# Attention loop of a block chain on one core: score matmuls ahead of the maximum ring, whole value sums, the shift in four tiles

## The chip, the core and the metric

The kernel runs on one core of a Trainium2 chip. TensorE (PE in the profile, PEld for its weight loads) multiplies, VectorE (DVE) reduces and normalises, ScalarE (ACT) applies exponentials and moves tiles out of PSUM, GpSimd (POOL) and SyncE (SP) do the rest. The metric is the time of one execution on the device in microseconds; lower is better. The median of three runs of the kernel before is 976.74 us (974.82 to 978.44).

## The reference

Eight residual blocks in a row work on x of 2 x 1024 tokens by 128 channels, in float32. The change touches only the softmax attention with rotary positions, 16 heads of 8 channels:

```
x_norm = layer_norm(x, g1, beta1)
q = (x_norm @ Wq + bq).reshape(B, S, H, hd).transpose(0, 2, 1, 3)
k = (x_norm @ Wk + bk).reshape(B, S, H, hd).transpose(0, 2, 1, 3)
v = (x_norm @ Wv + bv).reshape(B, S, H, hd).transpose(0, 2, 1, 3)
q = apply_rope(q); k = apply_rope(k)
q = q * (1.0 / jnp.sqrt(jnp.float32(hd)))
scores = jnp.einsum('bhqd,bhkd->bhqk', q, k)
attn = jax.nn.softmax(scores, axis=-1)
out = jnp.einsum('bhqk,bhkd->bhqd', attn, v)
...
x = x + attn_out
```

The other blocks (linear attention, two channel mixes, a top-2 and two top-1 expert layers, a linear memory) are the same in both kernels.

## The kernel before: how the attention loop is laid out

The class is SoftmaxAttention. Its work is cut into 16 **halves** (HALVES): one batch, one group of 4 heads (HG) and 512 queries each. A half runs through 8 **waves** (kt, 0 to 7), one for each tile of 128 keys. A wave k has these parts:

- **Scores.** Four matmuls (score, L1674), one for each head j = 0 to 3, of 32 rows of the array (rows 32j to 32j+31) and 512 columns in f16. Score tiles go round three PSUM banks (SCORE_BANKS, banks 4 to 6). score_bank makes PE wait on prob_in until ScalarE has read the tile three places earlier in the stream of tiles. stream_tiles numbers them: s0, s1, s2, s3 of each wave, and the shift tiles between.
- **Exponentials.** ScalarE turns each score tile into probabilities (L1871), in order, and raises prob_in after each. Before a wave's first one it waits on wave_in until the buffer of three waves earlier (PROBS) has been summed.
- **Value sum.** wave (L1705) multiplies the probabilities of wave k - 2 (BEHIND) with the values, in float32, into bank 7: four heads side by side in column groups of 32. Before, it is done in two parts of 256 columns, one after scores 0 and 1, the other after scores 2 and 3; for kt = 0 it is one piece of 512.
- **The maximum ring.** For the softmax each query's maximum over the keys is found in advance, one half ahead. ring_fill (L1614) computes the scores of 128 queries against 1024 keys of one head by two matmuls of 512 columns into one of two slots (banks 0 and 1, or 2 and 3); VectorE reduces a slot (L1634) and raises ring_out. An item may be filled only when VectorE has read the item two places earlier. A half has 16 items, in the order of fills(), and the loop fills two a wave, AHEAD = 4 items in front. Items of kind "o" transpose finished outputs (L1640), two tiles each, and are read by a reciprocal and a multiplication; there are four of them.
- **The shift.** shift subtracts the maxima from the queries: in a score bank one f16 copy of 512 columns (L1684) and four float32 matmuls of 128 columns (L1686, two passes each). ScalarE moves the result to qT2 (L1858). Before, that is done once a half, after wave kt = 6 (SHIFT_AT).
- **The sum's move.** After wave kt = 1 ScalarE copies the last half's sum out of bank 7 (move_sum, L1853); the first value sum of a half waits for it.

PE runs its instructions in the order that loop_tensor writes out. In it a wave is: ring item, s0, s1, first part of the sum, ring item, s2, s3, second part of the sum. keep_busy issues dummy matmuls (L287) whose results nobody reads. Ahead of the loop PE fills 2 ring items, then eight times one dummy, eight small transposes (turn_split, L1723) and 2 ring items. In the last half the transposes and projections of batch 0 and the late outputs of batch 1 are put between the waves.

## Time and profile before

| what | value |
|---|---|
| median of 3 runs | 976.74 us (974.82 to 978.44) |
| the profiled execution | 985.43 us, of which 983.5 us are its span |
| attention loop, from the first exponential to the last | 377.2 to 708.7 us of the span |
| TensorE busy | 861.3 us (88%) |
| VectorE busy | 665.9 us (68%) |
| ScalarE busy | 558.2 us (57%) |

In the profile a start is in us from the span's start, and a row of the timeline has its start, the time that it covers, engine, line, operation, output and input, shapes and the count of merged instructions; what stands in brackets is the engine's idle time ahead of it and who ended that. A matmul in float32 has two rows, one for each pass. Matmuls in different row groups of 32 can run side by side, so that durations overlap: what counts is the distance between starts.

### The profile page before, as it was taken

The page shows a single profiled execution, that of the slowest core. Times are in us where ns is not written, and L with a number is a line of the kernel's source. Part 1 is how long each engine was busy: PE and PEld are TensorE (multiplying, and loading weights), DVE is VectorE, ACT ScalarE, POOL GpSimd, SP SyncE. Part 2 cuts the span into 40 slices and gives each one's busy share as a digit, 9 for nine tenths or more (in the row PEclk, how much of TensorE's full clock was granted, in tenths as well). Part 3 has the DMA queues.
Part 4 walks back from the last instruction along what each step waited for, and adds up shares of the span by engine and source line. Part 5 has one row for each costly group of instructions (what it writes and reads, how often), then busy time and mean ns, then how long its engine had stood idle before and what let it go on. Part 6 is the DMA issues. An engine that isn't in the chain of part 4 may idle for free.

```text
span 983.5 us, 17217 instructions
## 1 busy us (share of the span) xinstructions
PE 861.3 (88%) x6571; PEld 536.4 (55%) x6571; DVE 665.9 (68%) x1248; ACT 558.2 (57%) x1188; POOL 198.1 (20%) x177
## 2 busy tenths in 40 slices
PE   4889935899988689999999999999996899895894
PEld 2579733599855443333333333333465599594694
DVE  5845882366487988999999888896335354566362
ACT  2442532165534836999989877889754055324152
POOL 2000047255400040000000000000030645104385
PEclk9999957999999968999999999999998799995798
DMA  5740001411120000000000000000060121100434
GB/s 118 201 129 1 2 19 51 123 37 34 42 80 1 1 1 1 2 1 2 1 1 2 2 2 1 1 2 1 2 172 2 61 69 37 43 2 25 125 34 70
DMA packets 54643, 36.86 MB, mean 37 GB/s; under 512 B 9138, under 2 KB 50162, under 8 KB 54546
## 3 DMA queue, kind: packets, MB, share of 16 engines
q1 hardware_dynamic: 47218, 25.98, 9.5%
q0 software_dynamic: 7344, 9.77, 4.3%
q8 instruction: 53, 0.87, 0.4%
q14 instruction: 28, 0.23, 0.1%
HBM read 22.31 MB, written 14.48 MB: 37 GB/s over the span
## 4 chain that ended last, share of the span: by engine, by line
PE 46%; DVE 20%; issue 19%; POOL 8%; DMA 3%; ACT 3%; SPq 1%; POOLq 0%; DVEq 0%; ACTq 0%
PE psum L1705 10%; DVE arena L1634 10%; PE psum L1614 8%; POOL results L1158 5%; PE psum L287 4%; PE psum L1674 3%; POOL results L1169 2%; PE psum L1251 2%; PE psum L402 2%; PE psum L380 2%; POOL slots L1147 2%; PE psum L1686 2%; PE psum L1766 1%; PE psum L1754 1%; PE psum L440 1%
## 5 line engine op out<-in xcount | busy, mean ns | idle before, releaser
L1634 DVE TENSOR_REDUCE arena<-psum 128x1 f32<-128x1024 f32 x256 | 296.8, 1219 | 33.9 <-PE psum L1614 30.8
L1871 ACT ACTIVATE arena<-psum 128x512 f32<-128x512 f32 x512 | 273.0, 599 | 32.9 <-PE psum L1674 24.5
L1294 ACT ACTIVATE arena<-psum,arena 128x128 f32<-128x128 f32 x340 | 96.9, 368 | 123.3 <-PE psum L1261 66.1
L1614 PE MATMUL psum<-arena 32*128 32x512 f16 x512 | 152.5, 388 | 8.3 <-ACT arena L1986 4.5
L1705 PE MATMUL psum<-arena 128*32 128x256 f32 (+1 forms) x1920 | 159.4, 405 | 0.2 <-ACT expert_w L1853 0.2
L1674 PE MATMUL psum<-arena 32*128 32x512 f16 x512 | 150.0, 385 | 0.5 <-ACT arena L1871 0.5
L287 PE MATMUL psum<-la_wqkv,ident 128*128 128x384 f32 x308 | 117.3, 532 | 7.2 <-issue 6.5
L1147 POOL DMA_INDIRECT slots<-xn,arena x64 | 66.3, 1036 | 196.1 <-DVE arena L1371 177.5
L1251 PE MATMUL psum<-arena 128*128 128x128 f32 x680 | 96.2, 286 | 1.4 <-DVE arena L1452 1.3
L287 PEld LDWEIGHTS psum<-la_wqkv,ident 128*128 128x128 f32 x308 | 60.9, 206 | 58.5 <-issue 25.6
L1261 PE MATMUL psum<-arena 128*128 128x128 f32 x680 | 90.4, 276 | 1.0 <-issue 0.7
L1251 PEld LDWEIGHTS psum<-arena 128*128 128x128 f32 x680 | 85.5, 197 | 4.7 <-DVE arena L1452 3.3
L1442 DVE COPY arena<-expert_w 128x1028 f32 x85 | 60.8, 715 | 35.9 <-issue 34.9
L1261 PEld LDWEIGHTS psum<-arena 128*128 128x128 f32 x680 | 83.4, 193 | 1.6 <-issue 1.1
L1614 PEld LDWEIGHTS psum<-arena 32*128 32x128 f16 x512 | 28.4, 93 | 101.8 <-DVE arena L1634 71.3
L1158 POOL DMA_INDIRECT results<-arena x62 | 61.6, 994 | 80.4 <-DVE arena L1457 78.6
L2158 POOL TENSOR_TENSOR x<-x,xn 128x1024 f32<-128x1024 f32 x2 | 4.7, 2358 | 362.6 <-DVE arena L2133 362.6
L1705 PEld LDWEIGHTS psum<-arena 128*32 128x32 f32 x1920 | 38.2, 108 | 71.5 <-issue 62.1
L1674 PEld LDWEIGHTS psum<-arena 32*128 32x128 f16 x512 | 42.3, 91 | 44.9 <-ACT arena L1871 32.3
L1457 DVE TENSOR_SCALAR arena<-psum,arena 128x128 f32<-128x128 f32 x85 | 29.8, 350 | 34.7 <-PE psum L1261 34.4
L1216 PE MATMUL psum<-arena 128*128 128x117 f32 (+1 forms) x128 | 23.4, 368 | 26.0 <-DVE arena L1397 26.0
L1169 POOL DMA_INDIRECT results<-arena x23 | 37.9, 1649 | 20.7 <-DVE arena L1457 14.0
(276 smaller groups left out, 1048.1 us busy)
## 6 DMA issues: line engine op xcount, KB each, us to landing
arena<-slots SPq DMA_DIRECT2D x19, 256.0 KB, 3.1
arena<-results SPq DMA_DIRECT2D x12, 256.0 KB, 4.0
slots<-blank SPq DMA_DIRECT2D x1, 2560.0 KB, 11.5
expert_w<-in_L_attn_b_w_dram SPq DMA_DIRECT2D x1, 2048.0 KB, 8.5
expert_w<-in_L_attn_b_w_dram SPq DMA_DIRECT2D x8, 256.0 KB, 4.8
expert_w<-in_L_ffn_W_dram SPq DMA_DIRECT2D x1, 2048.0 KB, 8.5
expert_w<-in_L_ffn_W_dram SPq DMA_DIRECT2D x8, 256.0 KB, 5.0
results<-arena POOLq DMA_INDIRECT x85
```

The costliest lines, as they stand in the source:

```text
L287: core.nc.tensor.matmul(core.psum[:, bank, 0:3 * D], w.ident[:, :], w.la_wqkv[:, :, :], start=True, stop=True)
L1147: pool.indirect_dma_start(out=self.slots[:, :], out_offset=bass.IndirectOffsetOnAxis(ap=self.slot_int[:, 0, at:at + 1], axis=0), in_=core. ...
L1158: pool.indirect_dma_start(out=self.results[:, :], out_offset=bass.IndirectOffsetOnAxis(ap=self.place_int[:, t:t + 1], axis=0), in_=self.y[ ...
L1251: last = nc.tensor.matmul(ps[:, 2 + p, c * P:(c + 1) * P], own[:, c * P:(c + 1) * P], self.xgT[:, p, :], start=True, stop=True)
L1261: last = nc.tensor.matmul(ps[:, 4 + p, 0:D], self.hT[:, p, c, :], own[:, c * D:(c + 1) * D], start=(c == 0), stop=(c == FC - 1))
L1294: last = nc.scalar.activation(self.hT[:, p, c, :], ps[:, 2 + p, c * P:(c + 1) * P], self.func, bias=own[:, FF + c:FF + c + 1])
L1442: v.tensor_copy(self.own[:, t % self.HELD, :], self.ew.all[:, bass.ds(at, EW)]).then_inc(self.copied, 1)
L1614: last = nc.tensor.matmul(core.psum[:, 2 * slot + keys, :], self.qT[rows, g, q0:q0 + P], self.kT[rows, g, k0:k0 + 512], start=True, stop=True)
L1634: v.tensor_reduce(self.m4[:, h % 2, qt, 32 * j + 24:32 * j + 25], core.psum[:, 2 * slot:2 * slot + 2, :], AX.XY, ALU.max).then_inc(self.ri ...
L1674: self.core.nc.tensor.matmul(self.score_bank(pe, self.tile_of["score", k, j]), self.kT[rows, g, at:at + P], self.qT2[rows, h % 2, :], star ...
L1705: last = nc.tensor.matmul(core.psum[32 * j:32 * j + 32, 7, cols], self.vs[:, b * TB + kt, HG * g + j, :], self.prob[:, k % self.PROBS, j, ...
L1871: nc.scalar.activation(self.prob[:, k % self.PROBS, j, :], core.psum[:, 4 + tile % self.SCORE_BANKS, :], ACT.Exp).then_inc(self.prob_in, 1)
```

## The change

- **Scores ahead of the ring.** A wave is now: s0, s1, ring item, the whole value sum of wave k - 2, s2, s3, the remaining ring items. For kt = 2 the sum stands at the end.
- **Whole sums.** The two parts of 256 columns are one piece of 512 in every wave.
- **Shift by tiles.** It is cut into four tiles of 128 queries, after waves kt = 1, 3, 5 and 6, each with its own score tile, its own wait for the ring and its own small move by ScalarE.
- **Halved outputs.** An "o" item holds one token tile; there are eight, two in each of four halves.
- **Dummies in front.** Six dummies before the first ring items and four after them are new; the eight between the splits shrink from 384 to 256 columns. In the loop the dummies of waves 0 and 1 stand once a wave.
- **The last half.** beside_last spreads the projections over waves 2 to 5 (two matmuls each) and the late outputs over waves 4 to 7; its one dummy goes.

```diff
-    SHIFT_AT = 6
+    SHIFT_AT = (1, 3, 5, 6)
...
+        out = self.score_bank(pe, self.tile_of["shift", h, q])[:, 0:P]
+        pe.wait_ge(self.ring_out, self.tile_read[h, q])
+        nc.tensor.matmul(out, self.w.ident16[:, :], self.qT[:, g, at:at + P], start=True, stop=False)
+        nc.tensor.matmul(out, self.m4[:, h % 2, q, :], self.turner, start=False, stop=True).then_inc(self.score_in, 1)
...
         for j in range(HG):
-            last = nc.tensor.matmul(core.psum[32 * j:32 * j + 32, 7, cols], self.vs[:, b * TB + kt, HG * g + j, :],
-                                    self.prob[:, k % self.PROBS, j, cols], start=(kt == 0), stop=(kt == TB - 1 and part == 1))
+            last = nc.tensor.matmul(core.psum[32 * j:32 * j + 32, 7, :], self.vs[:, b * TB + kt, HG * g + j, :],
+                                    self.prob[:, k % self.PROBS, j, :], start=(kt == 0), stop=(kt == TB - 1))
...
+        first = self.t[0]["qkT"][0]
+        core.moved(pe, first)
+        keep_busy(core, self.w, pe, first.bank, 6)
...
+        core.claim(pe, self.t[1]["qkT"][0])
+        keep_busy(core, self.w, pe, self.t[1]["qkT"][0].bank, 4)
...
-            keep_busy(core, self.w, pe, self.t[1]["qkT"][i].bank, 1)
+            keep_busy(core, self.w, pe, self.t[1]["qkT"][i].bank, 1, 2)
...
+            if kt == 0:
+                pe.wait_ge(self.prob_in, self.tile_of["shift", h, 3] + 1)
+            self.score(pe, k, 0)
+            self.score(pe, k, 1)
             if a < after:
                 self.ring_fill(pe, a)
                 a += 1
...
-            self.score(pe, k, 0)
-            self.score(pe, k, 1)
             if kt != self.BEHIND:
-                self.wave(pe, k - self.BEHIND, 0)
-            if k == 0:
+                self.wave(pe, k - self.BEHIND)
+            if k < 2:
                 keep_busy(core, self.w, pe, 7, 1)
+            self.score(pe, k, 2)
+            self.score(pe, k, 3)
             while a < after:
                 self.ring_fill(pe, a)
                 a += 1
-            self.score(pe, k, 2)
             if kt == self.BEHIND:
-                self.wave(pe, k - self.BEHIND, 0)
-            self.score(pe, k, 3)
-            self.wave(pe, k - self.BEHIND, 1)
...
-            if kt == self.SHIFT_AT and h + 1 < self.HALVES:
-                self.shift(pe, h + 1)
+                self.wave(pe, k - self.BEHIND)
+            if kt in self.SHIFT_AT and h + 1 < self.HALVES:
+                self.shift(pe, h + 1, self.SHIFT_AT.index(kt))
...
-        self.core.nc.scalar.copy(self.qT2[:, h % 2, :], self.core.psum[:, 4 + tile % self.SCORE_BANKS, :]
-                                 ).then_inc(self.prob_in, 1)
+        self.core.nc.scalar.copy(self.qT2[:, h % 2, q * P:(q + 1) * P],
+                                 self.core.psum[:, 4 + tile % self.SCORE_BANKS, 0:P]).then_inc(self.prob_in, 1)
```

On PE in the middle of a half, two waves of the kernel before (L1614 ring item, L1674 scores, L1705 a part of the sum):

```order
L1614 MATMUL psum<-arena 128x512 [waits sa_ring_out]
L1614 MATMUL psum<-arena 128x512
L1674 MATMUL psum<-arena 128x512 [waits sa_prob_in] x2
L1705 MATMUL psum<-arena 32x256 x4
L1614 MATMUL psum<-arena 128x512 [waits sa_ring_out]
L1614 MATMUL psum<-arena 128x512
L1674 MATMUL psum<-arena 128x512 [waits sa_prob_in] x2
L1705 MATMUL psum<-arena 32x256 [waits sa_prob_in]
L1705 MATMUL psum<-arena 32x256 x3
```

The same place now, with a shift tile at the end of the wave (L1678 scores, L1615 ring item, L1702 the sum, L1688 and L1689 the shift):

```order
L1678 MATMUL psum<-arena 128x512 [waits sa_prob_in] x2
L1615 MATMUL psum<-arena 128x512 [waits sa_ring_out]
L1615 MATMUL psum<-arena 128x512
L1702 MATMUL psum<-arena 32x512 [waits sa_prob_in]
L1702 MATMUL psum<-arena 32x512 x3
L1678 MATMUL psum<-arena 128x512 [waits sa_prob_in] x2
L1615 MATMUL psum<-arena 128x512 [waits sa_ring_out]
L1615 MATMUL psum<-arena 128x512
L1688 MATMUL psum<-arena,ident 128x128 [waits sa_ring_out,sa_prob_in]
L1689 MATMUL psum<-arena 128x128
```

Each pair of scores has moved ahead of its ring item, the whole sum stands between the second score and the third, and two ring items follow each other with no sum between them.

On ScalarE, the stretch from one sum's move to the next before (L1858 the shift's move, L1871 exponentials, L1853 the sum's move):

```order
L1853 COPY expert_w<-psum 128x512
L1871 ACTIVATE arena<-psum 128x512 x20
L1858 CAST arena<-psum 128x512
L1871 ACTIVATE arena<-psum 128x512 x12
L1853 COPY expert_w<-psum 128x512
```

The same stretch now (L1860, L1874 and L1855):

```order
L1855 COPY expert_w<-psum 128x512
L1874 ACTIVATE arena<-psum 128x512 x8
L1860 CAST arena<-psum 128x128
L1874 ACTIVATE arena<-psum 128x512 x8
L1860 CAST arena<-psum 128x128
L1874 ACTIVATE arena<-psum 128x512 x4
L1860 CAST arena<-psum 128x128
L1874 ACTIVATE arena<-psum 128x512 x12
L1860 CAST arena<-psum 128x128
L1855 COPY expert_w<-psum 128x512
```

One move of 512 columns has become four of 128, each in the stream of score tiles.

## Rows read from the trace of the kernel before

**Rows 1.** Stretches: us, busy time (count) by engine, clock, DMA share, GB/s

```profile
300.00:320.00 20.00, 17.01 (x66) 10.27 (x64) 16.57 (x67) 8.12 (x10) 0.00 (x0) 1.00 0.00 0
340.00:360.00 20.00, 13.79 (x57) 6.47 (x58) 16.28 (x22) 8.76 (x10) 12.22 (x6) 0.57 0.00 0
440.00:460.00 20.00, 19.82 (x203) 6.65 (x201) 18.70 (x18) 18.19 (x36) 0.00 (x0) 1.00 0.00 1
```

**Rows 2.** Timeline, PE and its weight loads within one ordinary wave

```profile
525.16 0.38 PE L1614 MATMUL psum<-arena 32*128 32x512 f16 x1
...
525.32 0.09 PEld L1674 LDWEIGHTS psum<-arena 32*128 32x128 f16 x1
525.39 0.37 PE L1614 MATMUL psum<-arena 32*128 32x512 f16 x1
...
525.69 0.64 PE L1705 MATMUL psum<-arena 128*32 128x256 f32 x8
...
526.54 0.09 PEld L1674 LDWEIGHTS psum<-arena 32*128 32x128 f16 x1 [0.17 <-ACT arena L1871]
```

**Rows 3.** Timeline of the same wave, single instructions of ScalarE, then of VectorE

```profile
525.89 0.60 ACT L1871 ACTIVATE arena<-psum 128x512 f32<-128x512 f32 x1
526.39 0.59 ACT L1871 ACTIVATE arena<-psum 128x512 f32<-128x512 f32 x1
...
525.80 1.22 DVE L1634 TENSOR_REDUCE arena<-psum 128x1 f32<-128x1024 f32 x1
528.07 1.22 DVE L1634 TENSOR_REDUCE arena<-psum 128x1 f32<-128x1024 f32 x1
```

**Rows 4.** Timeline at kt = 2, where the sum is whole already, and its scores

```profile
521.68 1.07 PE L1705 MATMUL psum<-arena 128*32 128x512 f32 x8
522.68 0.39 PE L1674 MATMUL psum<-arena 32*128 32x512 f16 x2
523.07 0.09 PEld L1674 LDWEIGHTS psum<-arena 32*128 32x128 f16 x1
...
522.34 0.67 ACT L1871 ACTIVATE arena<-psum 128x512 f32<-128x512 f32 x1
523.10 0.60 ACT L1871 ACTIVATE arena<-psum 128x512 f32<-128x512 f32 x1
```

**Rows 5.** Timeline around one shift, after kt = 6

```profile
532.20 1.05 PE L1686 MATMUL psum<-arena 128*128 128x128 f32 x8
...
533.29 0.58 ACT L1858 CAST arena<-psum 128x512 f16<-128x512 f32 x1 [0.73 <-PE psum L1686]
...
533.83 1.23 DVE L1634 TENSOR_REDUCE arena<-psum 128x1 f32<-128x1024 f32 x1 [1.13 <-PE psum L1614]
```

**Rows 6.** Timeline, the shift's move in two ordinary halves and two with "o" items

```profile
493.92 0.58 ACT L1858 CAST arena<-psum 128x512 f16<-128x512 f32 x1 [0.73 <-PE psum L1686]
513.54 0.58 ACT L1858 CAST arena<-psum 128x512 f16<-128x512 f32 x1 [0.73 <-PE psum L1686]
597.60 0.58 ACT L1858 CAST arena<-psum 128x512 f16<-128x512 f32 x1 [0.70 <-PE psum L1686]
620.59 0.58 ACT L1858 CAST arena<-psum 128x512 f16<-128x512 f32 x1 [0.70 <-PE psum L1686]
```

**Rows 7.** Timeline ahead of the loop: PE, and ScalarE's first exponentials

```profile
343.88 1.04 PE L1614 MATMUL psum<-arena 32*128 32x512 f16 x4 [4.48 <-ACT arena L1986]
...
350.62 1.65 PE L287 MATMUL psum<-la_wqkv,ident 128*128 128x384 f32 x2
...
354.09 1.65 PE L287 MATMUL psum<-la_wqkv,ident 128*128 128x384 f32 x2
...
377.20 1.08 ACT L1871 ACTIVATE arena<-psum 128x512 f32<-128x512 f32 x2
```

**Rows 8.** Timeline of the last half, ScalarE's exponentials of two waves

```profile
700.73 2.06 ACT L1871 ACTIVATE arena<-psum 128x512 f32<-128x512 f32 x4 [0.98 <-PE psum L1674]
703.59 2.06 ACT L1871 ACTIVATE arena<-psum 128x512 f32<-128x512 f32 x4 [0.80 <-PE psum L1674]
```

More of the change, by code:

```diff
@@ L281, in transpose_tiles, with keep_busy @@
     last.then_inc(core.filled[turn.bank], 1)
-def keep_busy(core, w, pe, bank, times):
+def keep_busy(core, w, pe, bank, times, blocks=3):
     for _ in range(times):
-        core.nc.tensor.matmul(core.psum[:, bank, 0:3 * D], w.ident[:, :], w.la_wqkv[:, :, :], start=True, stop=True)
+        core.nc.tensor.matmul(core.psum[:, bank, 0:blocks * D], w.ident[:, :], w.la_wqkv[:, 0:blocks, :], start=True,
+                              stop=True)
 class LinearAttention:
@@ L1552, in __init__ @@
         self.last_of = {item[1]: a for a, item in enumerate(self.order) if item[0] == "max"}
+        self.tile_read = {(item[1], item[2][0]): a + 1 for a, item in enumerate(self.order) if item[0] == "max"}
         self.o_turns = {}
@@ L1575, in fills @@
                 order.append(("max", h, part))
-                if i == 8 and self.EARLY + 2 <= h < self.EARLY + 6:
-                    order.append(("o", h - self.EARLY - 2, None))
+                if i in (4, 12) and self.EARLY + 2 <= h < self.EARLY + 6:
+                    order.append(("o", 2 * (h - self.EARLY - 2) + i // 8, None))
         return order
     def stream_tiles(self):
-        tiles = [("shift", 0, None)]
+        tiles = [("shift", 0, q) for q in range(4)]
         for k in range(TB * self.HALVES):
@@ L1675, in score, with shift, wave @@
                                    self.qT2[rows, h % 2, :], start=True, stop=True).then_inc(self.score_in, 1)
-    def shift(self, pe, h):
+    def shift(self, pe, h, q):
         nc = self.core.nc
         b, g, half = self.half_of(h)
-        at = b * S + 512 * half
-        out = self.score_bank(pe, self.tile_of["shift", h, None])
-        pe.wait_ge(self.ring_out, self.last_of[h] + 1)
-        nc.tensor.matmul(out, self.w.ident16[:, :], self.qT[:, g, at:at + 512], start=True, stop=False)
-        for q in range(4):
-            last = nc.tensor.matmul(out[:, q * P:(q + 1) * P], self.m4[:, h % 2, q, :], self.turner, start=False,
-                                    stop=(q == 3))
-        last.then_inc(self.score_in, 1)
-    def wave(self, pe, k, part):
+        at = b * S + 512 * half + q * P
+        out = self.score_bank(pe, self.tile_of["shift", h, q])[:, 0:P]
+        pe.wait_ge(self.ring_out, self.tile_read[h, q])
+        nc.tensor.matmul(out, self.w.ident16[:, :], self.qT[:, g, at:at + P], start=True, stop=False)
+        nc.tensor.matmul(out, self.m4[:, h % 2, q, :], self.turner, start=False, stop=True).then_inc(self.score_in, 1)
+    def wave(self, pe, k):
         core, nc = self.core, self.core.nc
@@ L1740, in project @@
                                          self.w.sa_wo[:, :], start=True, stop=True)
-        last.then_inc(core.filled[turn.bank], 1)
+        if half != 0:
+            last.then_inc(core.filled[turn.bank], 1)
     def turn_second(self, pe, b):
@@ L1796, in loop_tensor @@
         pe.wait_ge(self.pads, 7)
-        self.shift(pe, 0)
+        for q in range(4):
+            self.shift(pe, 0, q)
         waves = TB * self.HALVES
```

93 lines of the change are left out of this document (42 added, 51 removed).

## The prediction

> **What bounds the kernel now.** I first read the stretches of 20 us and looked for the engine that is never free. In an ordinary stretch of the loop PE is busy 19.82 of 20 us, VectorE 18.70 and ScalarE 18.19, at the full clock of 2.4 GHz [rows 1]. All three are nearly full, so neither busy times nor one engine's wait settles what an edit is worth; the order in which they hand tiles to each other does. So I went to the timeline of one wave. VectorE starts two reads in 2.27 us (525.80 to 528.07) [rows 3], back to back: a floor of 8 x 2.27 = 18.2 us for a half of 16 items. A half takes 19.62 us (493.92 to 513.54) [rows 6]; most of the difference is the shift, at which VectorE stands idle 1.13 us and ScalarE 0.73 us [rows 5].
>
> The second thing to see is the loop over the three score banks. Score 1 of a wave takes the bank of score 2 of the wave before and can't start until ScalarE has read it. An exponential that starts at 525.89 lets the waiting weight load go at 526.54: 0.65 us [rows 2, 3]. At kt = 2 the one from 522.34 (0.67 us long) lets the load at 523.07 go [rows 4]. This loop turns in 2.27 us too, since only half a sum lies between score 1 and score 2.
>
> **The change, part by part.**
>
> *Whole sum between score 1 and score 2.* I follow the bank loop through the new order, from the start x of score 1.
> - The ring item starts beside it, in another row group; its second matmul starts 0.23 us later, as 525.16 to 525.39 [rows 2].
> - The sum starts 0.30 us after that, as 525.39 to 525.69 [rows 2].
> - Score 2 starts 1.00 us after the start of a whole sum: 521.68 to 522.68 [rows 4].
> - Its exponential starts 0.42 us after the score: 522.68 to 523.10, a score with no ring item to finish before it [rows 4].
> - The next wave's score 1 follows 0.65 us after that start [rows 2, 3].
>
> Together 0.23 + 0.30 + 1.00 + 0.42 + 0.65 = 2.60 us for a wave, against 2.27. Nothing in it can be hidden: score 1 blocks PE's queue, and behind it stand the ring item, the sum, and scores 2 and 3. That scores go ahead of the ring does help, since their results are out earlier (already in the 0.42), but it also puts the ring behind a bank's wait. PE's own work falls: 0.23 + 0.30 + 1.00, then the second ring item with 0.23 and 0.23 more until its row group is free, 1.99 us. VectorE needs 2.27. Both fit into 2.60, and both now wait.
>
> *The shift by tiles.* A shift tile after score 3 moves the stream by one place: score 1 of the next wave then needs the bank of score 3, not of score 2. Score 3's exponential comes 0.49 us after score 2's (525.89 to 526.39) [rows 3]. So each of four waves in a half takes 2.60 + 0.49 = 3.09. The PE work of a tile, a copy and two passes of 128 columns (eight passes take 1.05 us [rows 5]) with a change of tiling at each side, is some 0.7 us; it lies in PE's wait of 3.09 - 1.99 = 1.1 us. The ring items that it waits for are read by then, two or more behind the newest. ScalarE's small move hides in ScalarE's spare time (four exponentials need some 2.0 us, as in 2.06 for four [rows 8]). At kt = 2 the sum stands last: score 3 needs the first exponential, which is behind score 3's of wave 1, the small move and the sum's move. That is x - 0.65 + 0.49 + 0.25 + 0.47 + 0.65 = x + 1.21, then 0.01 + 0.23 + 0.30 + 1.00, so 2.75, taken as 2.80 (0.25 and 0.47 are bounded by 0 and the 0.49 of an exponential).
>
> A half: 3 x 2.60 + 4 x 3.09 + 2.80 = 22.96 us, against 19.62: **+3.34**. Halves 1 to 8, 13 and 14 are of this kind: 10 x 3.34 = **+33.4**.
>
> *Halved outputs.* Halves 9 to 12 hold them and take 22.99 us before (597.60 to 620.59) [rows 6]. After, the "o" items fall behind score 3, into PE's wait: nothing. Items out of step put the ring's first matmul in score 1's own row group twice a half: 2 x 0.23. So 22.96 + 0.46 = 23.4, **+2.0** for four halves (0 to 6: from no conflict at all to an "o" item that doesn't fit).
>
> *Half 0.* Waves 0 and 1 hold a dummy in place of the sum, before and after, and ran partly at the half clock: **+1**.
>
> *Last half.* No ring: 0.30 + 1.00 + 0.42 + 0.65 = 2.37 us a wave, and three of the eight stretched to 2.8 to 3.0 by projections and transposes: 20.5. Before, such a wave takes 2.86 (700.73 to 703.59) [rows 8], the half 22.3. **-1.8** (-3 to +1).
>
> *Dummies in front.* The first ring items wait 4.48 us with PE idle, and the clock in 340 to 360 is 0.57 [rows 1, 7]: a stretch mostly at 1.2 GHz. Units of dummy, split and two ring items come 3.47 us apart there (350.62 to 354.09) [rows 7]; VectorE's floor for two items is 2.27. With ten dummies in the two gaps the clock should be high earlier: four units nearer to 2.4 save 4 us, shorter dummies 0.5, a fast first shift and first wave 1.5; four small moves and some remaining half clock take 1 back: **-5** (0 if the clock isn't raised, -8 at most). The dummies stand in gaps, so they cost nothing.
>
> Sum: 33.4 + 2.0 + 1.0 - 1.8 - 5.0 = **+29.6 us**. The profiled execution has 985.43 us, of which 983.5 are span, and would become 1015.0; it is 8.7 us above the median of 976.74. I take the difference over: 976.7 + 29.6 = **1006.3 us**. If each of the 110 affected waves is off by 0.05, that is 5.5 us; with the ends of the front the forecast's own range is 998 to 1016.
>
> **The rivals.**
>
> *The bank loop doesn't decide* (faster). If score 2 reached ScalarE early enough, VectorE's 2.27 would pace the waves and the shift would no longer stop it: 18.4 us a half. Ten halves by -1.2, four by -3.4 (22.99 to 19.6), front -5: -31, so 946. For it: PE's work of 1.99 and the gaps in [rows 5]. It decides if a wave's way from score 1 to score 2 is under 1.2 us; I find 0.23 + 0.30 + 1.00 = 1.53. Chance 0.13.
>
> *The bank loop decides but is shorter* (about the same). If score 2 could start while the sum's last columns drain, the wave might be 2.40 and a shift wave 2.70: a half 20.5, ten by +0.9, four by -2.2, front and last half -6.8: -7 to 0, about 973. Against it stands the start at 522.68 only after the whole sum [rows 4]. The step between this and the forecast belongs here too. Chance 0.09, of which a third ends at 984 or more.
>
> *The clock falls* (slower still). PE now waits 0.6 of each 2.6 us. At 17.01 busy of 20 the clock was 1.00, at 13.79 it was 0.57 [rows 1]; the changed loop lies nearer to the first. At 1.2 GHz the PE steps double: 0.4 + 0.4 + 2.0 + 0.6 + 0.65 = 4.05 a wave, +1.45. Three halves so: 24 x 1.45 = +35, giving 1041. The Trainium skill, page "TensorE: Matmul & The Clock Gate", section "A second HAM failure mode: psum-queue depth-cycling", tells of a kernel that went round its PSUM banks in each iteration and idled briefly between groups of matmuls, and whose clock swung for it; by that rule this change could give the 1041. In the trace of before, which also goes round its banks but hardly idles, the loop holds 1.00. Chance 0.08.
>
> **How the numbers follow.** The forecast has 0.70, faster 0.13, about the same 0.09, clock 0.08. The likeliest is 1006.3. A range from 985 to 1030 holds the forecast's case, the upper part of the third and half of the clock's: about 0.78. A difference within 0.5%, 972 to 982, is about what a measurement can't tell from none. Faster by over 0.5%: 0.13 + 0.01 = 0.14; within: 0.05; slower: 0.70 + 0.08 + 0.03 = 0.81.
>
> **What would show it.** Right: exponentials of the ordinary halves in waves of 2.6 and 3.1 us, half after half some 23.0 us; the waits name PE's score weight load behind ScalarE's exponential as the largest, VectorE behind the ring item on PE next; VectorE busy near 16 of 20 us. Front: first exponential near 372 in place of 377.20 and fewer units at the half clock. Wrong: halves of 18 to 19 us with VectorE full, or score 2 starting less than 1.2 us after score 1; a granted clock under 1.00 in the loop would be the third rival.

## The result, and the profile after

| what | before | after |
|---|---|---|
| median (fastest to slowest) | 977.59 us (974.82 to 993.73, 4 runs) | 1074.80 us (1061.86 to 1099.75, 4 runs) |
| the profiled execution, and its span | 985.43, 983.5 us | 1099.75, 1097.8 us |
| loop, first to last exponential | 377.2 to 708.7 us | 371.4 to 824.0 us |
| an ordinary half | 19.63 us | 22.88 us |

The ratio is 1.092 (95% interval 1.080 to 1.105): slower, and by some 97 us where 29.6 were forecast; it lies outside the range. The executions of the changed kernel differ in how long TensorE ran at 1.2 GHz, and the profiled one is the longest of the four, so its sizes are read beside the others below. Every ratio in this text compares only those executions of two kernels that lie within about 1.5% of the fastest of their own kernel, while a median is of all executions.

The page of the kernel after: TensorE's row, then the clock granted in 40 slices of 27 us, then the costliest groups (busy us, mean ns | idle us ahead of them and who ended it).

```profile
PE 965.0 (88%) x5739; PEld 529.9 (48%) x5739; DVE 677.9 (62%) x1256; ACT 559.0 (51%) x1236; POOL 198.2 (18%) x177
...
PEclk9999768999989589999998555555989879997798
...
L1634 DVE TENSOR_REDUCE arena<-psum 128x1 f32<-128x1024 f32 x256 | 307.7, 1223 | 123.2 <-PE psum L1615 122.6
L1874 ACT ACTIVATE arena<-psum 128x512 f32<-128x512 f32 x512 | 273.2, 604 | 156.8 <-PE psum L1678 156.3
```

The busy time of ScalarE is as it was (559.0 against 558.2 us) and that of VectorE is 12 us longer. VectorE now waits for PE 123 us and ScalarE 156 us. The row of digits shows what the busy times hide: six slices at 5, half speed, in the middle of the loop. The waits in the loop (us in total, times, longest) name the circle of the prediction, exponentials behind scores and score weights behind exponentials:

```profile
ACT arena L1874 <- PE psum L1678: 156.3, 151, 3.5
PEld psum L1678 <- ACT arena L1874: 153.9, 237, 1.7
DVE arena L1634 <- PE psum L1615: 119.8, 172, 2.6
```

The same view of before, 377 to 709 us:

```profile
PEld psum L1674 <- ACT arena L1871: 32.3, 112, 1.0
DVE arena L1634 <- PE psum L1614: 26.2, 31, 1.6
ACT arena L1871 <- PE psum L1674: 24.5, 59, 1.0
```

One wave of after with a shift tile, PE's part of the timeline. It is the answer to [rows 2, 4]:

```profile
437.42 0.39 PE L1678 MATMUL psum<-arena 32*128 32x512 f16 x1 [0.25 <-ACT arena L1874]
437.42 0.60 PE L1615 MATMUL psum<-arena 32*128 32x512 f16 x2
437.95 1.07 PE L1702 MATMUL psum<-arena 128*32 128x512 f32 x8
438.95 0.39 PE L1678 MATMUL psum<-arena 32*128 32x512 f16 x2
...
440.52 0.60 PE L1615 MATMUL psum<-arena 32*128 32x512 f16 x2
```

Score 1 waits for ScalarE (0.25 us) and starts at 437.42; the sum follows 0.53 us later (0.23 + 0.30), scores 2 and 3 another 1.00 later, and the next wave's ring item, which goes with its score 1, comes 3.10 us after this one. ScalarE there, its exponentials and the shift's small move:

```profile
439.37 1.08 ACT L1874 ACTIVATE arena<-psum 128x512 f32<-128x512 f32 x2 [0.54 <-PE psum L1678]
440.35 0.27 ACT L1860 CAST arena<-psum 128x128 f16<-128x128 f32 x1
440.51 1.10 ACT L1874 ACTIVATE arena<-psum 128x512 f32<-128x512 f32 x2
```

438.95 to 439.37 is the 0.42 of the prediction. The sum's move (L1855) in two successive halves, at the full clock, counts a half (duration ns, first and last start):

```profile
L1855 ACT COPY expert_w<-psum x2: 616/616/616, 451.9 to 474.8; 128x512 f32<-128x512 f32 x2
```

22.9 us. Then the stretches of 20 us of after: us, busy time (count) of PE, PEld, DVE, ACT, POOL, clock, DMA share, GB/s.

```profile
360.00:380.00 20.00, 19.53 (x65) 7.35 (x65) 12.52 (x12) 9.38 (x19) 0.00 (x0) 0.52 0.00 0
420.00:440.00 20.00, 18.31 (x123) 4.22 (x122) 17.01 (x15) 15.68 (x34) 0.00 (x0) 1.00 0.00 1
600.00:620.00 20.00, 19.98 (x77) 5.09 (x77) 9.17 (x10) 9.34 (x19) 0.00 (x0) 0.50 0.00 0
760.00:780.00 20.00, 18.64 (x117) 3.89 (x109) 15.23 (x13) 13.21 (x29) 0.00 (x0) 0.92 0.00 1
```

At 420 to 440 PE and VectorE both have idle time, as the forecast has it for the full clock. From 600 PE is busy 19.98 of 20 us at the clock 0.50, and the other two do half as much. The clock's records of this execution give one spell at 1.2 GHz of 167.3 us from 596.1 (halves 9 to 13), one of 23.9 us from 360.6 (its last 13 us in half 0), and in the other halves spells of 3.4 or 6.8 us, one in about every second half: 204 us of the loop. In the loop of before it is 3.3 us, all of it in half 0.

**Where the time went.** The starts of the exponentials give each half:

| half | 0 | 1 to 8 | 9 | 10 to 12 | 13 | 14 | 15 |
|---|---|---|---|---|---|---|---|
| before | 21.45 | 19.63 each (one 19.75) | 22.66 | 22.99 each | 19.96 | 19.00 | 21.69 |
| after | 26.74 | 22.88 four times, 24.5 three times, 25.48 | 34.69 | 41.35, 41.35, 41.56 | 29.71 | 22.45 | 23.76 |
| after, with no spell (estimate) | 21.6 | 22.88 | 24.2 | 25.3 each | 22.9 | 22.45 | 20.7 to 21.7 |

The last row takes for each half a stretch at 2.4 GHz, from this trace or from the experiments below. Halves 1 to 8 and 14 are this trace's. Half 0 is e6's, which has the same code there. Halves 9 to 12 are an estimate from kernels whose code differs a little: e6 has its outputs side by side (24.20 and 25.27), e3 its ring first (25.37). Half 13 is taken as an ordinary one. For half 15 the bounds are e1's 21.71, with dummies and no spell, and e12's 22.33, less some 1.6 us for the 3.4 us at 1.2 GHz in it.

The row adds to some 371 to 372 us. By another way: e1's loop takes 394.4 us; less 6.5 for its dummies, and less some 14 for its 34 us at 1.2 GHz, that is 374. The loop before has 331. So of the +121.1 us of the loop (452.6 against 331.5) **40 to 43 are the new order** at the full clock, and **78 to 81 are the clock**. The loop starts 5.8 us earlier (371.44 against 377.20 [rows 7]). 121.1 - 5.8 = 115.3, and the two profiled executions differ by 114.3. In the four executions of after the span goes with the time at 1.2 GHz (twice the span times what the clock lacks of 1): 223, 255, 271 and 327 us with spans of 1059.9, 1069.4, 1076.4 and 1097.8, which is 0.36 us for each us so spent. By the medians, 34 to 37 of the 97 us belong to the order and the front and some 60 to the clock; this is an estimate, since it takes the profiled executions' order and front over to the others.

### The profile page after: what moved, and what is told of

It reads as the page before. It is cut to its first block, busy times and chain, and to the rows that moved or that the text cites. A ratio compares the mean times of both kernels' runs of the same rounds, so it can differ in the third digit from the quotient of the medians.

```text
span 1097.8 us, 15660 instructions
## 1 busy us (share of the span) xinstructions
PE 965.0 (88%) x5739; PEld 529.9 (48%) x5739; DVE 677.9 (62%) x1256; ACT 559.0 (51%) x1236; POOL 198.2 (18%) x177
## 4 chain that ended last, share of the span: by engine, by line
PE 54%; POOL 12%; DVE 10%; issue 10%; ACT 9%; DMA 4%; SPq 1%; POOLq 0%; DVEq 0%; ACTq 0%
PE psum L1702 15%; PE psum L1678 9%; PE psum L1615 7%; ACT arena L1874 6%; POOL slots L1148 6%; POOL results L1159 4%; POOL results L1170 2%; PE psum L1252 2%; PE psum L403 1%; PE psum L381 1%; DVE arena L1634 1%; PE psum L1765 1%; PE psum L1753 1%; PE psum L280 1%; PE psum L1262 1%
## 5 line engine op out<-in xcount | busy, mean ns | idle before, releaser
L1634 DVE TENSOR_REDUCE arena<-psum 128x1 f32<-128x1024 f32 x256 | 307.7, 1223 | 123.2 <-PE psum L1615 122.6
L1874 ACT ACTIVATE arena<-psum 128x512 f32<-128x512 f32 x512 | 273.2, 604 | 156.8 <-PE psum L1678 156.3
L1615 PE MATMUL psum<-arena 32*128 32x512 f16 x512 | 183.0, 459 | 5.6 <-DVE arena L1634 4.9
L1702 PE MATMUL psum<-arena 128*32 128x512 f32 x1024 | 173.2, 757 | 0.0
L1678 PE MATMUL psum<-arena 32*128 32x512 f16 x512 | 148.1, 452 | 21.0 <-ACT arena L1874 15.2
L1678 PEld LDWEIGHTS psum<-arena 32*128 32x128 f16 x512 | 32.7, 94 | 225.5 <-ACT arena L1874 153.9
L287 PE MATMUL psum<-la_wqkv,ident 128*128 128x384 f32 (+1 forms) x324 | 116.4, 512 | 2.4 <-ACT arena L1974 2.0
L1159 POOL DMA_INDIRECT results<-arena x62 | 61.6, 994 | 74.9 <-DVE arena L1458 73.6
L1702 PEld LDWEIGHTS psum<-arena 128*32 128x32 f32 x1024 | 22.1, 118 | 69.0 <-ACT arena L1874 43.2
L1615 PEld LDWEIGHTS psum<-arena 32*128 32x128 f16 x512 | 33.6, 100 | 27.7 <-DVE arena L1634 14.1
L1217 PE MATMUL psum<-arena 128*128 128x117 f32 (+1 forms) x128 | 24.2, 376 | 25.9 <-DVE arena L1398 25.9
L1453 DVE COPY arena<-psum 128x128 f32<-128x128 f32 x85 | 24.0, 282 | 35.9 <-PE psum L1243 35.9
```

Of the source, the lines that this page charges most:

```text
L287: core.nc.tensor.matmul(core.psum[:, bank, 0:blocks * D], w.ident[:, :], w.la_wqkv[:, 0:blocks, :], start=True, stop=True)
L1159: pool.indirect_dma_start(out=self.results[:, :], out_offset=bass.IndirectOffsetOnAxis(ap=self.place_int[:, t:t + 1], axis=0), in_=self.y[ ...
L1615: last = nc.tensor.matmul(core.psum[:, 2 * slot + keys, :], self.qT[rows, g, q0:q0 + P], self.kT[rows, g, k0:k0 + 512], start=True, stop=True)
L1634: v.tensor_reduce(self.m4[:, h % 2, qt, 32 * j + 24:32 * j + 25], core.psum[:, 2 * slot:2 * slot + 2, :], AX.XY, ALU.max).then_inc(self.ri ...
L1678: self.core.nc.tensor.matmul(self.score_bank(pe, self.tile_of["score", k, j]), self.kT[rows, g, at:at + P], self.qT2[rows, h % 2, :], star ...
L1702: last = nc.tensor.matmul(core.psum[32 * j:32 * j + 32, 7, :], self.vs[:, b * TB + kt, HG * g + j, :], self.prob[:, k % self.PROBS, j, :], ...
```

## The experiments

Four questions, one after the other: is the order worth what the sum said; which part makes it; what makes the clock fall; and what do the front and the outputs do. "Ordinary half" is always one at the full clock, from the starts of the exponentials; "spells" are the times at 1.2 GHz in the profiled execution. In each group all diffs are against the kernel named.

### The order at the full clock

**e7: whole sums alone**, on the kernel before.

```diff
             if kt != self.BEHIND:
-                self.wave(pe, k - self.BEHIND, 0)
+                self.wave(pe, k - self.BEHIND)
...
             self.score(pe, k, 3)
-            self.wave(pe, k - self.BEHIND, 1)
```

> The kernel before with whole value sums and nothing else. Bank loop theory: 0.30 + 1.00 from score 1 to the ring item behind the sum, 0.23 more until score 2's result can follow it, 0.42 and 0.65: 2.60 us a wave in place of 2.27; a half 8 x 2.60 and 0.49 for the one shift tile, less what kt = 2 had already: 21.3 to 21.7 us in place of 19.63, halves 9 to 12 25 to 26; 1003 to 1012 us if the clock holds, more by the spells if it falls. Rival (whole sums save TensorE time, and the shift tiles cost): halves of 19 us, 965 to 970 us.

Measured 1002.5 us (1000.13 to 1018.94), ratio 1.024 (1.0215 to 1.0266). Three sum's moves, so two halves, in 43.3 us, 21.65 each:

```profile
L1846 ACT COPY expert_w<-psum x3: 593/593/593, 441.7 to 485.0; 128x512 f32<-128x512 f32 x3
```

As forecast: the longer piece between score 1 and score 2 alone costs 2.0 us a half. Halves 9 to 12 took 23.9 to 24.1 us, less than the 25 to 26 expected. Its loop has no spell at all.

**e2: the sum in two parts again**, everything else of after.

```diff
             if kt != self.BEHIND:
-                self.wave(pe, k - self.BEHIND)
+                self.wave(pe, k - self.BEHIND, 0)
...
+            self.wave(pe, k - self.BEHIND, 1)
```

> The changed kernel with the value sum in two parts of 256 columns again, one behind each ring item; scores stay ahead of the ring, the shift in tiles, the dummies in front. Bank loop theory: from score 1 to score 2 are 0.23 + 0.30 + 0.57 = 1.10 us, the loop is 2.17 and VectorE's 2.27 paces an ordinary wave; a shift wave takes 2.17 + 0.49 = 2.66. A half is 4 x 2.27 + 4 x 2.66 = 19.7 us, TensorE hardly waits, the clock holds at 1.00; halves 9 to 12 near 20.5 in place of 22.99; in all 960 to 968 us. Rival (the order, scores ahead of the ring, is what costs): halves stay near 22.9 us and the time over 1000.

Measured 1009.91 us (984.10 to 1053.20). Five moves are four halves, 81.5 us, 20.37 each:

```profile
L1862 ACT COPY expert_w<-psum x5: 592/592/592, 453.2 to 534.7; 128x512 f32<-128x512 f32 x5
```

So 2.5 of the 3.25 us that a half grew are the whole sum. But the time missed: 960 to 968 us were expected, with the clock at 1.00. The wide spread goes with the clock: the fastest execution, with a mean clock of 0.95, lies 7 us above the fast ones of before, and the profiled one has a spell of 160 us, below. So the long spell does not need the whole sum.

**e8: the shift by tiles alone**, and **e10: scores ahead of the ring alone**, both on before.

```diff
-    SHIFT_AT = 6
+    SHIFT_AT = (1, 3, 5, 6)
```

> The kernel before with the shift in four tiles after kt = 1, 3, 5 and 6 and nothing else; ring first, sums in two parts. Bank loop theory: an ordinary wave stays at 2.27 us, a wave behind a shift tile takes 2.17 + 0.49 = 2.66 or a little over, the single stop of 1.21 us goes: halves of 20.2 to 20.5 us against 19.63, so about 8 to 12 us slower in all, 985 to 990 us. Rival (the tiles give VectorE's idle 1.1 us back): halves of 18.5 to 19 us, 962 to 970 us.

```diff
-            if a < after:
-                self.ring_fill(pe, a)
-                a += 1
...
             self.score(pe, k, 1)
+            if a < after:
+                self.ring_fill(pe, a)
+                a += 1
...
             self.score(pe, k, 3)
+            while a < after:
+                self.ring_fill(pe, a)
+                a += 1
             self.wave(pe, k - self.BEHIND, 1)
```

> The kernel before with the two scores of each half wave ahead of the ring's item and nothing else; sums in two parts, one shift. Bank loop theory: from score 1 to score 2 are 1.10 us, the loop is 2.17 and VectorE's 2.27 paces: halves of 19.5 to 19.8 us, the time within 3 us of the kernel before. Rival (scores ahead of the ring cost by themselves): halves of 20.5 us and more, over 985 us.

e8 measured 997.78 us (979.14 to 1012.32), ratio 1.003 (0.997 to 1.010), and 19.86 us a half: less than the 20.2 to 20.5 expected, since its shift waves of 2.71 are partly made good by ordinary ones of 2.2. e10 measured 994.93 us (979.64 to 1001.28), ratio 1.006 (0.997 to 1.015), and 19.85 a half, where 19.5 to 19.8 were expected. Each part alone costs 0.2 us, while a whole sum added 2.0: the shift tile's 0.49 lies on the path only where the bank loop already sets the wave.

**e3: after, with the ring item ahead of the scores again.**

```diff
-            self.score(pe, k, 0)
-            self.score(pe, k, 1)
             if a < after:
                 self.ring_fill(pe, a)
                 a += 1
+            self.score(pe, k, 0)
+            self.score(pe, k, 1)
...
-            self.score(pe, k, 2)
-            self.score(pe, k, 3)
             while a < after:
                 self.ring_fill(pe, a)
                 a += 1
+            self.score(pe, k, 2)
+            self.score(pe, k, 3)
```

> The changed kernel with the ring item ahead of its two scores again in both half waves; whole sums, shift tiles and dummies in front stay. Bank loop theory: the sum starts 0.30 us after score 1 in place of 0.53, but score 2's result comes 0.23 later, after the ring item's: 2.60 us a wave as before, so halves of 22.9 us and the same 1055 to 1080 us. Rival (the order of scores and ring is what costs): halves near 19.6 to 21 and under 1000 us.

Measured 1060.01 us (1036.35 to 1076.49), ratio 1.067 (1.052 to 1.083), and 23.08 a half. The order that gives the change its name saves 0.2 us a half here; nothing of the loss comes from it.

**e13: after, with the sum at the wave's end** (s0, s1, ring item, s2, ring items, s3, whole sum).

```diff
-            if kt != self.BEHIND:
-                self.wave(pe, k - self.BEHIND)
...
             self.score(pe, k, 2)
-            self.score(pe, k, 3)
             while a < after:
                 self.ring_fill(pe, a)
                 a += 1
-            if kt == self.BEHIND:
-                self.wave(pe, k - self.BEHIND)
+            self.score(pe, k, 3)
+            self.wave(pe, k - self.BEHIND)
```

> The changed kernel with the whole sum behind score 3 (scores 0 and 1, ring item, score 2, ring items, score 3, sum); the same matmuls. Bank loop theory: score 3 follows score 0 by 0.42 + 0.65 = 1.07 us, the sum by 0.30 more and the next score 0 by 1.00: 2.37 us an ordinary wave in place of 2.60, near 3.07 with a shift tile, 21.8 us a half in place of 22.88, more of TensorE's time in use, so fewer spells at the half clock: 990 to 1040 us. Rival (the whole sum costs where it is put no matter): halves of 22.9 us.

Measured 1028.99 us (1021.17 to 1032.58), ratio 1.050 (1.044 to 1.057). Six moves are five halves, 108.1 us, 21.62 each:

```profile
L1852 ACT COPY expert_w<-psum x6: 591/592/592, 444.2 to 552.3; 128x512 f32<-128x512 f32 x6
```

The bank loop's sum gave 2.37 and 3.07 a wave; 2.45 and 2.88 to 2.89 were measured (3.15 in the one wave that also has the sum's move). The account by starts holds for an order of which no trace had been seen, and halves 1 to 8 have no spell.

### The clock

**e1: after, with a dummy ahead of score 0** in every wave from the third on, 128 columns in float32, into the bank that score 0 will take.

```diff
+            if k >= 2:
+                bank = self.tile_of["score", k, 0]
+                self.score_bank(pe, bank)
+                keep_busy(core, self.w, pe, 4 + bank % self.SCORE_BANKS, 1, 1)
             self.score(pe, k, 0)
```

> The changed kernel with one more dummy matmul of 128 columns a wave, written into the bank of the next score 0 just ahead of it, where TensorE otherwise waits for the score banks. Clock theory (the bank loop costs 30 us and all above that is time at 1.2 GHz, which TensorE's waits bring on): the dummy fills the waits, the granted clock of the loop is near 1.00, halves 1 to 8 stay at 22.9 us, halves 9 to 12 come to 23.4 to 24, and the time to 1003 to 1012 us. Rival (halves 9 to 12 are slow by their own order, and the clock is a companion): the time stays above 1050 us. Rival (dummies cost more than they give): halves of over 24 us at a clock of 1.00.

Measured 1037.68 us (1026.08 to 1046.83), ratio 1.053 (1.046 to 1.061). The page's clock row, then the stretch 600 to 620:

```profile
PEclk9999868999999659999998999998999699997798
```

```profile
600.00:620.00 20.00, 19.09 (x126) 6.59 (x125) 15.57 (x15) 14.21 (x29) 0.00 (x0) 1.00 0.00 1
```

The row of fives is gone; 34 us of the loop are left at 1.2 GHz (17 of them in half 0) in place of 204. The dummies make the ordinary half longer, 23.29 in place of 22.88, and halves 9 to 12 take 25.4 to 26.2, where 23.4 to 24 were expected. The time expected, 1003 to 1012 us, was missed by 26 us: the halves with outputs were priced too low, and some spells stay. Yet **more work on PE took 37 us off the time**, and the intervals of the two ratios (1.046 to 1.061, and 1.080 to 1.105) don't touch: the clock is a cause of its own, and the order a second one, since 52 us stay against the median of before beside it (985.70). The size fits: by their mean clocks the median execution of after spends 263 us of its span at 1.2 GHz and that of e1 142; 121 x 0.36, less 6.5 for the dummies, is 37.

**e12: the same dummy only in halves 9 to 12.**

```diff
+            if 9 <= h < 13:
+                bank = self.tile_of["score", k, 0]
+                self.score_bank(pe, bank)
+                keep_busy(core, self.w, pe, 4 + bank % self.SCORE_BANKS, 1, 1)
```

> The changed kernel with a dummy of 128 columns ahead of each score 0 in halves 9 to 12 alone. Clock theory: the long spell at the half clock goes, halves 9 to 12 take 25 to 26.5 us in place of 35 to 41, ordinary halves stay at 22.9 with a short spell now and then; 1020 to 1045 us. Rival (the ordinary halves' waits bring the long spell on in any case): one spell of over 100 us remains, over 1055 us.

Measured 1058.47 us (1043.64 to 1065.42), ratio 1.071 (1.062 to 1.080). Two stretches, one without dummies and one with:

```profile
540.00:560.00 20.00, 19.74 (x82) 4.03 (x78) 11.03 (x10) 11.12 (x23) 0.00 (x0) 0.50 0.00 0
...
640.00:660.00 20.00, 19.43 (x131) 6.76 (x124) 15.81 (x15) 13.03 (x27) 0.00 (x0) 1.00 0.00 1
```

Where the dummies stand the clock is 1.00 through halves 9 to 12; where they don't, a spell of 44 us took halves 6 and 7 and one of 24 us half 13. In this one profiled execution the spells stand exactly where the dummies don't, as expected. The time expected was missed by 13 us at the median, since I had put nearly all of the clock's loss in halves 9 to 12, and the others can fall as well.

**e5: outputs paired as before**, and **e6: two halved outputs side by side**, both on after. They ask if the outputs make the spell, by their form or because they put the items out of step.

```diff
-                if i in (4, 12) and self.EARLY + 2 <= h < self.EARLY + 6:
-                    order.append(("o", 2 * (h - self.EARLY - 2) + i // 8, None))
+                if i == 8 and self.EARLY + 2 <= h < self.EARLY + 6:
+                    order.append(("o", h - self.EARLY - 2, None))
```

> The changed kernel with the outputs in pairs again, one paired item in each of four halves as before. From the end of each paired item to the next one the ring is out of step with the scores (its item uses the row group of a score beside it). Out-of-step theory (it is the ring out of step that lowers the granted clock for long): the halves out of step still fall to 1.2 GHz, 1040 to 1080 us. Rival (the halved outputs themselves, eight times a change of tiling, bring the clock down): no spell of over 30 us at the half clock, 1010 to 1030 us.

```diff
-                if i in (4, 12) and self.EARLY + 2 <= h < self.EARLY + 6:
-                    order.append(("o", 2 * (h - self.EARLY - 2) + i // 8, None))
+                if i == 8 and self.EARLY + 2 <= h < self.EARLY + 6:
+                    order.append(("o", 2 * (h - self.EARLY - 2), None))
+                    order.append(("o", 2 * (h - self.EARLY - 2) + 1, None))
```

> The changed kernel with the two halved outputs of a half side by side, after the ring's item 8, so that the ring is never out of step for longer than they last. Out-of-step theory: halves 9 to 12 take 23.5 to 24.5 us at the full clock, no spell of over 30 us at the half clock, 1012 to 1035 us with the short spells of the other halves. Rival (any output item in a loop with waits brings the clock down): halves 10 to 12 at 35 to 41 us, and over 1055 us.

e5 measured 1089.0 us (1074.89 to 1102.27), ratio 1.104 (1.095 to 1.114): no better than after, with spells of 44 and 96 us. e6 measured 1066.4 us (1040.66 to 1077.27), against 979.52 of before beside it, 30 us or more over what was expected. It has no spell over 44 us (106 us in all), and two stretches that look alike:

```profile
540.00:560.00 20.00, 19.74 (x82) 3.38 (x81) 12.08 (x10) 10.87 (x22) 0.00 (x0) 0.50 0.00 0
600.00:620.00 20.00, 18.67 (x122) 5.23 (x122) 15.76 (x17) 15.35 (x32) 0.00 (x0) 1.00 0.00 1
```

So the form of the outputs is not the cause: paired as before, they leave the spells. The theory that the ring out of step makes them isn't borne out either, since e6 in step missed its time by 31 us. Where the spells stand differs between the three kernels, and with one profile of each that can't be told from chance.

**What goes with the falls.** From the profiled executions (e14 and e4, whose loops are those of before, left out):

| kernel | ordinary half, us | at 1.2 GHz in halves 1 to 8, us | halves 9 to 12 at 2.4 GHz, us | their longest spell, us |
|---|---|---|---|---|
| before | 19.63 | 0 | 22.7 to 23.0 | 0 |
| e9 | 19.63 | 0 | 23.3 to 23.6 | 0 |
| e10 | 19.85 | 0 | 22.8 to 23.1 | 0 |
| e8 | 19.86 | 0 | 23.0 to 23.1 | 0 |
| e2 | 20.37 | 0 | 24.3 | 160 |
| e13 | 21.62 | 0 | 24.5 | 6.8 |
| e7 | 21.65 | 0 | 23.9 to 24.1 | 0 |
| after | 22.88 | about 17 | 24.2 to 25.3 | 167 |
| e3 | 23.08 | about 14 | 25.4 to 25.6 | 120 |
| e5, e6, e12 | 22.88 | 58 to 61 | e5 24.3 (96 us), e6 24.2 to 25.3 (14) | e12, with dummies: 0 |
| e1, dummies | 23.29 | about 10 | 25.4 to 26.2 | 0 |

The work on PE in a half is nearly the same in all but the last row; the longer a half, the more PE waits in it. Halves up to 21.7 us never fell, those of 22.9 and more did in five kernels of five without dummies, and of the halves with outputs those from about 24.3 us on did in most. It is an order of sizes, not a law: e13 and e2 have about the same length there and fared differently. The dummies in front are not what brings the spells on: e4, e9 and e14 have them, and none has a spell in halves 1 to 15. PE's busy share doesn't do as a measure. e7 in 600 to 620:

```profile
600.00:620.00 20.00, 16.97 (x118) 4.99 (x116) 16.97 (x15) 14.88 (x30) 0.00 (x0) 1.00 0.00 1
```

and e2 ahead of its spell and in it:

```profile
520.00:540.00 20.00, 19.41 (x196) 5.60 (x192) 18.29 (x17) 18.25 (x37) 0.00 (x0) 1.00 0.00 1
...
600.00:620.00 20.00, 20.00 (x105) 5.02 (x103) 10.20 (x10) 8.95 (x17) 0.00 (x0) 0.50 0.00 1
```

16.97 of 20 held the full clock, and 18.31 in after had falls among its halves. What in a wave decides stays **open**.

### The front and the outputs alone

**e4 and e14: the kernel before with the front's dummies**, the same kernel on two occasions.

```diff
+        first = self.t[0]["qkT"][0]
+        core.moved(pe, first)
+        keep_busy(core, self.w, pe, first.bank, 6)
...
+        core.claim(pe, self.t[1]["qkT"][0])
+        keep_busy(core, self.w, pe, self.t[1]["qkT"][0].bank, 4)
...
-            keep_busy(core, self.w, pe, self.t[1]["qkT"][i].bank, 1)
+            keep_busy(core, self.w, pe, self.t[1]["qkT"][i].bank, 1, 2)
```

> The kernel before with the dummies in front alone (six, four, and the eight of 256 columns in place of 384). Front theory: the first exponential starts near 371.5 us in place of 377.2, the loop is unchanged with halves of 19.63, so 970 to 973 us. Rival (the front only moves the half clock to another place): 975 to 979.

> The kernel before with the dummies in front alone, once more. In an execution of the order-alone kernel, whose front is that of the kernel before, TensorE ran at 1.2 GHz from the front through the whole of half 0, which took 32.2 us in place of 20 to 21. Front theory: such executions are what makes a third to a half of the runs of the kernel before 993 to 1004 us long; with the dummies none falls so: all runs from 967 to 985 us, a median of 974 to 978 beside 977 to 986 for the kernel before. Rival (chance, which the first ten runs happened to miss): a third of the runs over 990 us.

e4: 977.26 us (969.41 to 984.25, 10 runs), ratio 1.001 (0.997 to 1.005). e14: 980.89 us (975.55 to 984.85, 12 runs), ratio 1.002 (0.9995 to 1.005). In e4's profile the stretch that was 13.79 us busy at 0.57 [rows 1] is

```profile
340.00:360.00 20.00, 18.81 (x111) 9.21 (x112) 19.84 (x24) 8.98 (x9) 12.22 (x6) 1.00 0.00 1
```

and the first exponential stands at 367.64 in place of 377.20. Yet most executions are no faster than those of before: e4's median is 977.26 us where 970 to 973 were expected, e14's 980.89 where 974 to 978 were. One reason is that 377.20 is a late start among those of before's front. The same front gave a first exponential at 372.12 in e7, 373.33 in e8 and 381.74 in e10, and the new front, in the eleven kernels that have it, 367.36 to 375.67. The means are 376.1 and 371.3, and the two ranges overlap. e14's profile shows one way in which the lead is lost: a spell of 31 us follows at once.

```profile
340.00:360.00 20.00, 18.62 (x95) 9.20 (x94) 18.33 (x25) 9.31 (x10) 12.23 (x6) 0.88 0.00 1
360.00:380.00 20.00, 20.00 (x72) 8.17 (x70) 12.86 (x11) 7.08 (x9) 0.00 (x0) 0.50 0.00 0
```

What the dummies do is cut off the long end: none of the 22 executions is over 985 us, while of before's beside the experiments 18 of 45 are over 990. e10 shows what such a long one is. It has the front of before, and a spell of 68 us went through its half 0, which took 32.2 us in place of 21.5:

```profile
340.00:360.00 20.00, 14.41 (x60) 6.60 (x60) 15.65 (x21) 8.73 (x10) 12.22 (x6) 0.57 0.00 0
360.00:380.00 20.00, 19.81 (x73) 9.12 (x71) 14.14 (x12) 4.63 (x6) 0.00 (x0) 0.50 0.00 1
380.00:400.00 20.00, 19.26 (x78) 3.79 (x78) 10.93 (x9) 11.70 (x21) 0.00 (x0) 0.50 0.00 1
```

**e9: e4 with the outputs halved and side by side.**

```diff
                 if i == 8 and self.EARLY + 2 <= h < self.EARLY + 6:
-                    order.append(("o", h - self.EARLY - 2, None))
+                    order.append(("o", 2 * (h - self.EARLY - 2), None))
+                    order.append(("o", 2 * (h - self.EARLY - 2) + 1, None))
```

> The kernel before with the dummies in front, and with halved outputs side by side after item 8, so that the ring stays in step. Halves 9 to 12 take 20.5 to 21.5 us in place of 22.99, all others as before; with the front 966 to 971 us. Rival (the paired output's cost is its transposes and not the step): halves of 22 to 23 us, as the dummies in front alone, 974 to 978.

Measured 981.64 us (975.18 to 983.25), ratio 1.002 (0.998 to 1.007). Halves 9 to 12 take 23.3 and 23.63 three times, against 22.99: a little longer and not the 20.5 to 21.5 of the theory. Two halved items side by side cost a half 4.0 us and one paired item 3.4, so halving them saves nothing here. How much of that is the place in the ring and how much the item's own work isn't separated.

No version that I ran beats the kernel before beyond the measurement.

## Why the prediction was right and wrong, point by point

- **What bounds the loop: right.** The bank loop of score tiles sets the wave. In an ordinary half of after the waves last 2.61, 3.23, 2.71, 2.61, 2.93, 2.77, 3.09 and 2.93 us. The single steps (0.23 + 0.30, 1.00, 0.42) stand in the timeline above as they were forecast, and the rival that it doesn't decide is out: 438.95 - 437.42 = 1.53 us, over the 1.2 at which it would have.
- **An ordinary half: right.** 22.96 forecast, 22.88 measured; ten of them +32.5 us at the full clock (+33.4).
- **Halves 9 to 12: too small.** +2.0 forecast, 6 at most; at the full clock some 24.2 + 3 x 25.3 = 100.1 against 91.6, so +8.5. The term that failed is the "o" items, which I put into PE's wait at no cost (with two conflicts of 0.23): against an ordinary half's 22.88 they cost 1.3 to 2.4 us a half. e9 shows without the new order that two halved items cost more than a paired one, 23.6 against 22.99.
- **Half 0:** +1 forecast. At the full clock 21.6 (e6), against 19.90 for the old loop (e4), so +1.7; the 21.45 of before has 3.3 us at 1.2 GHz in it.
- **Last half: gain too large or none.** -1.8 forecast. By the starts of the exponentials before has 21.69; after at the full clock is bounded by 20.7 and 21.7, so 0 to -1. The trace of after itself has 23.76, with a spell in it.
- **The front: near as a start, wrong as a gain.** First exponential 371.44 (forecast 372). That it is 5.8 us earlier is in part luck, since before's profiled execution started late; the means of the two fronts differ by 4.8 us. And e4 and e14 show that in most executions it gives nothing on the total.
- **Sum at the full clock:** +34 to +37 in place of +29.6, some 1011 to 1014 us, inside the range. The likeliest case would have held, though the parts that were off go both ways.
- **The clock: the step that failed.** I gave the fall 0.08 and three halves, on the ground that a stretch of 17.01 us busy had held 1.00 and one of 13.79 hadn't [rows 1]. The changed loop is busy 18.31 of 20, and still fell, in its ordinary halves and for 167 us from half 9. The busy share was the wrong measure; it was also a measure taken from other code. The rival's length was too short: three halves at 1.2 GHz, which at its price are 104 us, where 204 were measured. The sum and the scores of half 10 show the slow steps:

```profile
645.44 1.94 PE L1702 MATMUL psum<-arena 128*32 128x512 f32 x8
647.31 0.61 PE L1678 MATMUL psum<-arena 32*128 32x512 f16 x2
```

1.87 us from one to the other, in place of 1.00.

The rival's price a wave, 4.05 us and with a tile's 0.49 so 4.54, held outside the halves with outputs. In e12's spell in half 6, which has the same code as after, a wave with a tile goes so:

```profile
530.97 0.61 PE L1678 MATMUL psum<-arena 32*128 32x512 f16 x2
531.94 0.29 PE L1688 MATMUL psum<-arena,ident 128*128 128x128 f16 x1
532.69 0.66 PE L1678 MATMUL psum<-arena 32*128 32x512 f16 x2
533.71 1.93 PE L1702 MATMUL psum<-arena 128*32 128x512 f32 x8
535.58 0.61 PE L1678 MATMUL psum<-arena 32*128 32x512 f16 x2
```

From scores to scores that is 0.97 + 0.75 + 1.02 + 1.87 = 4.61 us, and waves without a tile took 3.80 to 4.20 there. An ordinary half put together from the waves at 1.2 GHz of e5, e6 and e12 (halves 6 and 7) takes 35.0 us, 12.1 more than at 2.4, where I had 11.6. In half 10 of after the same wave is longer:

```profile
652.15 0.61 PE L1678 MATMUL psum<-arena 32*128 32x512 f16 x2
652.55 1.06 PE L1615 MATMUL psum<-arena 32*128 32x512 f16 x2
653.54 0.29 PE L1688 MATMUL psum<-arena,ident 128*128 128x128 f16 x1
654.30 0.61 PE L1678 MATMUL psum<-arena 32*128 32x512 f16 x2
655.69 1.94 PE L1702 MATMUL psum<-arena 128*32 128x512 f32 x8
657.55 0.60 PE L1678 MATMUL psum<-arena 32*128 32x512 f16 x2
```

1.39 + 0.76 + 1.39 + 1.86 = 5.40 us. Here each ring item starts 0.40 us after its scores, where in e12 it starts with them (530.98 and 530.97), and the wave has two such items. That fits the conflict in one row group that the prediction names for items out of step, and prices at 0.23 twice a half; no run tests it by itself. Halves 10 to 12 took 16 us more than at 2.4 GHz. The long spell takes some 66 us in halves 9 to 13, the smaller ones 12 to 15, together the 78 to 81 of the profiled execution.

The section that the prediction named beside this rival, "A second HAM failure mode: psum-queue depth-cycling" of the page "TensorE: Matmul & The Clock Gate" in the Trainium skill, tells of a clock that swings when a kernel goes round its PSUM banks with short idle times of PE. This trace agrees with the swing: 204 us of the loop at 1.2 GHz, against 3.3 of before. It doesn't bear out that short idle times are what costs in the long spell, where PE is idle 0.02 of 20 us.

## What to carry to other kernels

Where a few PSUM banks go round between two engines, price an edit by the starts round that loop: a piece of work put between the last tile that waits for a bank and the next one counts in full, in every round (here 512 columns in place of 256, 2.0 to 2.5 us a half), while moves beside the loop cost 0.2. When an edit makes TensorE wait for more of each round, give the fall of the clock a real chance and take a long one into the range; and where a ring item may fall beside a score of its own row group, count that in every wave (here a wave took 5.40 us at half speed where it took 4.61 in step). A cheap test is a small dummy matmul at the wait, which here gave back 37 us of 97. A spread between executions that is larger than before can be the sign (1061.86 to 1099.75 here, and 984.10 to 1053.20 in e2).

## What the runs showed of the hardware

- The clock stayed at 1.2 GHz for 120 to 167 us within halves 9 to 14 (after, e2 and e3) with PE busy 19.98 (after) and 20.00 (e2) of 20 us, and came back in half 13 (after) or 14 (e2 and e3). A full PE didn't bring it back at once.
- A time at 1.2 GHz cost 0.36 us for each us in after (four executions), and some 0.39 by its halves 10 to 12 (16.0 more in 41.34); a spell of 3.4 us in an ordinary half cost 1.6.
- One dummy of 128 columns in float32 a wave held 1.00 where the same halves without it had fallen (e12, halves 9 to 12); in e1 it cost 0.41 us an ordinary half and left 34 us of the loop at 1.2 GHz in place of 204.
- Spells of 44 us in e5, e6 and e12 began at nearly the same place, half 6 (522.0, 520.5 and 526.1 us), while after had 3.4 us at 524.5. What the four share and what parts them I can't tell.
